# Second attention's stacks loaded as an image from DRAM, and the first expert-choice call's first half routed among the mixture's units

## The reference

```
x = x + 0.5 * mixture(LN(x))          # shared expert + top 2 of 8 experts, silu(g)*u, hidden 256
x = x + linear_attention(LN(x))       # 4 blocks
x = x + 0.5 * mixture(LN(x))          # the same weights again
x = x + 0.5 * expert_choice(LN(x))    # each of 8 experts takes 64 tokens of each sequence
x = x + causal_attention(LN(x))       # 16 heads of 8, rotation by the head's index
x = x + 0.5 * expert_choice(LN(x))
```

## Time and profile before

| | |
|---|---|
| median of 3 runs | 1073.49 us (1071.27 to 1079.22) |
| profiled execution | 1074.08 us |
| its span | 1072.4 us |
| mean granted clock of TensorE | 0.951 |
| busy: PE, DVE, ACT, POOL | 959.2, 706.4, 619.3, 338.7 us |

### The profile page before, as it was taken

One profiled execution on the slowest core, in us unless ns is written; L12 is line 12 of the kernel. 1 busy time (PEld: TensorE's weight loads), 2 busy tenths in 40 slices (PEclk: granted clock), 3 DMA queues, 4 the chain that ended last, 5 costly groups with the idle time before them and its releaser, 6 DMA issues.

```text
span 1072.4 us, 13356 instructions
## 1 busy us (share of the span) xinstructions
PE 959.2 (89%) x4674; PEld 636.4 (59%) x4674; DVE 706.4 (66%) x1413; ACT 619.3 (58%) x1003; POOL 338.7 (32%) x249
## 2 busy tenths in 40 slices
PE   8899999889999999889999998899977878787997
PEld 5678887333333333357888875688544545454886
DVE  3978887577877787546888877634375455438532
ACT  6555555378888888653555553635644545445454
POOL 1697777100000000003777764201201211123200
PEclk9999999999999999888999998899988888889999
DMA  5225120000000000004321211100000000001001
GB/s 173 50 76 162 60 66 23 0 0 1 1 1 1 0 1 1 0 1 135 76 67 59 63 37 60 40 2 1 1 2 2 4 2 2 4 1 40 1 1 40
DMA packets 30745, 33.66 MB, mean 31 GB/s; under 512 B 2063, under 2 KB 19799, under 8 KB 30679
## 3 DMA queue, kind: packets, MB, share of 16 engines
q1 hardware_dynamic: 30678, 32.81, 10.6%
HBM read 31.36 MB, written 1.18 MB: 30 GB/s over the span
## 4 chain that ended last, share of the span: by engine, by line
PE 50%; DVE 20%; ACT 11%; POOL 11%; issue 8%; DMA 0%; SPq 0%; ACTq 0%; POOLq 0%; DVEq 0%
POOL fl L2174 9%; PE ps L128 6%; PE ps L129 6%; PE ps L130 6%; PE ps L760 5%; PE ps L878 4%; PE ps L754 2%; ACT ex L1504 2%; ACT L1393 2%; PE ps L738 2%; DVE smax L2053 2%; PE ps L972 2%; PE ps L907 1%; DVE stk L2045 1%; PE ps L981 1%
## 5 line engine op out<-in xcount | busy, mean ns | idle before, releaser
L2174 POOL TENSOR_TENSOR fl<-fp,fh 128x512 fp32r<-128x512 f32 x144 | 224.1, 1573 | 123.5 <-ACT fh L1299 123.4
L1290 ACT ACTIVATE fs<-ps 128x512 f32<-128x512 f32 x144 | 86.3, 599 | 112.7 <-PE ps L130 112.5
L1762 DVE TENSOR_TENSOR fp<-fp,cwb 128x512 f32<-128x512 f32 x128 | 140.3, 1096 | 14.0 <-DVE fp L1755 0.9
L1755 DVE TENSOR_TENSOR fp<-fs,ps 128x512 f32<-128x512 f32 x144 | 98.1, 682 | 39.4 <-ACT fs L1290 39.0
L128 PE MATMUL ps<-z_hi,w_hi 128*128 128x512 f32 x288 | 116.4, 404 | 3.3 <-DVE fp L1755 3.3
L129 PE MATMUL ps<-z_lo,w_hi 128*128 128x512 f32 x288 | 115.7, 402 | 0.0
L130 PE MATMUL ps<-z_hi,w_lo 128*128 128x512 f32 x288 | 115.2, 400 | 0.0
L1299 ACT CAST fh<-fp 128x512 fp32r<-128x512 f32 x144 | 88.8, 617 | 35.4 <-DVE fp L1762 31.0
L2238 POOL TENSOR_TENSOR ln_sq<-ln_rs 128x512 f32<-128x512 f32 x20 | 21.4, 1069 | 264.8 <-ACT ln_rs L1356 264.8
L2231 POOL TENSOR_SCALAR_AFFINE_SELECT ex<-ex 128x1024 f32<-128x1024 f32 (+1 forms) x24 | 33.4, 1403 | 158.5 <-ACT ex L1504 158.5
L2053 DVE TENSOR_REDUCE smax<-ps 128x8 f32<-128x2048 f32 (+1 forms) x24 | 54.9, 2290 | 42.0 <-PE ps L986 33.9
(11 more groups left out here) (272 smaller groups left out, 2037.1 us busy)
## 6 DMA issues: line engine op xcount, KB each, us to landing
cwb<-cw_spread SPq DMA_DIRECT2D x64, 256.0 KB, 3.1
w_raw<-in_L_ffn_w_dram SPq DMA_DIRECT2D x20, 256.0 KB, 3.1
w_raw<-in_L_ffn_w_dram SPq DMA_DIRECT2D x4, 512.0 KB, 5.7
w<-in_L_ffn_w_dram SPq DMA_DIRECT2D x8, 256.0 KB, 4.8
x_tok<-in_L_attn_x_dram SPq DMA_DIRECT2D x4, 256.0 KB, 3.6
wb<-in_L_attn_W_dram SPq DMA_DIRECT2D x1, 1024.0 KB, 7.0
wb<-in_L_attn_W_dram SPq DMA_DIRECT2D x4, 256.0 KB, 3.9
out_dram<-z SPq DMA_DIRECT2D x4, 256.0 KB, 3.0
```

The costliest lines, as they stand in the source:

```text
L1290: act.activation(fs[:, n % 2, :], ps[:, n % 2, :], ACT.Silu).then_inc(silu_done, 1)
L1755: dve.tensor_tensor(f, fs[:, n % 2, :], ps[:, 2 + n % 2, :], ALU.mult).then_inc(prod_done, 1)
L1762: dve.tensor_tensor(f, f, cwb[:, x % CW_RING, :], ALU.mult).then_inc(weighed, 1)
L2174: pool.tensor_tensor(fl[:, n % RING0, :], fp[:, n % RING0, :], f32(fh[:, n % RING0, :]), ALU.subtract).then_inc(flo_done, 1)
```

## The change

Two parts, and a set-up that the second needs.

1. The routing of the first half of the first expert-choice call moves from the tail into the mixture's units of call 1. With EARLY1 = 47, PE issues the two centrings behind unit 47, the variances behind 50, the scores behind 51, the transposes of the probabilities behind 55, those of the gates and indices behind 67. ACT does one square and copy behind each of 48 and 49, and behind 53 a table load, the exp, and a table load back. DVE does root and weights behind 52, chances behind 54, top_start behind 56, one round behind each of 57 to 64, top_end behind 65, columns behind 68. In the tail the 28 fillers are gone, the two index matmuls stand behind the two turns, and ACT turns the rows of blocks 0 and 1 ahead of the squares of blocks 2 and 3.

2. For blocks 1 to 3 the eight steps are replaced. project_both makes q and k of a block with unscaled weights (wun): two mm3. ACT's both_high writes their high parts (hm), DVE's both_low their low parts (low_qk). SP stores these, as rows, into an image in DRAM (six stores of 256 KB a block: three PARTS for each n), and loads the image into the stack (two loads of 1 MB). The image's constant rows are stored once, from a blank made by POOL in stk[1]. both_high and both_low of blocks 2 and 3 wait until the stores of the block before have landed; plain of a block's first sequence waits for its load. The stores of a block wait for the load of the block before, and a load into a stack waits for the last reads of that stack.

3. In the first expert choice: a re-ordered copy of rope, two matmuls of one column, a copy of the bias and four strided copies 128x128 that make wun from wst.

```diff
+            def store_rows(tb):
+                sp.wait_ge(high_done, 2 * tb)
+                sp.wait_ge(low_done, 2 * tb)
+                if tb == 1:
+                    sp.wait_ge(blank_stored, 16 * 2)
+                else:
+                    sp.wait_ge(stk_loaded, 16 * 2 * (tb - 1))
+                for n in range(2):
+                    for k in range(PARTS):
+                        part = low_qk if k == LOW_PART[n] else hm
+                        sp.dma_start(stk_image[n].rearrange("(g c) h t -> g (c h) t", g=4)[:, HD * HG * k:HD * HG * (k + 1), :],
+                                     f32(part[:, n, :])).then_inc(rows_stored, 16)
+            def load_stack(tb):
+                sp.wait_ge(rows_stored, 16 * 2 * PARTS * tb)
+                if tb >= 2:
+                    sp.wait_ge(t_ready, 3 * SPB * (tb - 1))
+                for n in range(2):
+                    sp.dma_start(f32(stk[tb % 2][:, n]), stk_image[n]).then_inc(stk_loaded, 16)
+            sp.wait_ge(blank_done, 1)
+            for n in range(2):
+                sp.dma_start(stk_image[n], f32(stk[1][:, n])).then_inc(blank_stored, 16)
             for s in range(SEQS):
...
+                if s == 0:
+                    store_rows(1)
+                    load_stack(1)
+                elif s in (1, 3):
+                    store_rows((s + 3) // 2)
+                elif s in (2, 4):
+                    load_stack(s // 2 + 1)
...
+                def project_both(tb):
+                    for n in range(2):
+                        mm3(pe, ps[:, qk_bank(tb, n), :], wun_hi[:, n, :], wun_lo[:, n, :], blk(z_hi, tb), blk(z_lo, tb)).then_inc(both_ready, 1)
...
-                    if first and more:
-                        project_in(tb + 1, range(stack_mid(tb + 1), stack_mid(tb + 1) + 2))
+                    if first and tb + 2 < NTB:
+                        project_both(tb + 2)
...
-                        project_in(1, range(2))
+                        project_both(1)
...
-                    if first and more and tb > 0:
-                        pe.wait_ge(exp_done, 3 * s + 2)
-                        project_in(tb + 1, range(4, 8))
...
+                def both_high(tb):
+                    if tb == 1:
+                        act.wait_ge(stk_done, 2 * HG)
+                    else:
+                        act.wait_ge(rows_stored, 16 * 2 * PARTS * (tb - 1))
+                    for n in range(2):
+                        act.wait_ge(both_ready, 2 * (tb - 1) + n + 1)
+                        act.activation(hm[:, n, :], ps[:, qk_bank(tb, n), :], ACT.Identity, bias=bsu[:, n:n + 1]).then_inc(high_done, 1)
...
-                    if first and more:
-                        stack(tb + 1, range(stack_mid(tb + 1), stack_mid(tb + 1) + 4))
+                    if first and tb + 2 < NTB:
+                        both_high(tb + 2)
...
+                    if call == 1 and n == EARLY1 + 6:
+                        act.preload_act_table_set(LN_EXP)
+                        chances(0, 0)
+                        act.preload_act_table_set("silu_and_others")
...
+                    if call == 1 and n == EARLY1 + 5:
+                        dve.wait_ge(sc_ready, part1(0, 0) + 1)
+                        ln_root(LN_FFN1, 0, SPB - 1)
+                        part_weights(0, LN_FFN1, 0)
+                    if call == 1 and n == EARLY1 + 7:
+                        chances(0, 0)
+                    if call == 1 and n == EARLY1 + 9:
+                        top_start(0, 0)
+                    if call == 1 and n - EARLY1 - 10 in range(CAP // 8):
+                        top_rounds(0, 0, (n - EARLY1 - 10,))
+                    if call == 1 and n == EARLY1 + 18:
+                        top_end(0, 0)
+                    if call == 1 and n == EARLY1 + 21:
+                        columns(0, 0)
...
+                    for half, whole in ((wun_hi, wst_hi), (wun_lo, wst_lo)):
+                        for n in range(2):
+                            own.did(dve.tensor_copy(half[:, n, :].rearrange("p (g r h) -> p g r h", r=HD, h=HG),
+                                                    f32(whole[:, n, :]).rearrange("p (h g c) -> p g c h", h=HG, c=32)[:, :, 0:HD, :]))
...
+                def both_low(tb):
+                    if tb > 1:
+                        dve.wait_ge(rows_stored, 16 * 2 * PARTS * (tb - 1))
+                    for n in range(2):
+                        dve.wait_ge(high_done, 2 * (tb - 1) + n + 1)
+                        dve.scalar_tensor_tensor(out=low_qk[:, n, :], in0=ps[:, qk_bank(tb, n), :], scalar=bsu[:, n:n + 1],
+                                                 in1=f32(hm[:, n, :]), op0=ALU.add, op1=ALU.subtract).then_inc(low_done, 1)
...
+                pool.wait_ge(z_ready, NTB * HALVED.index(LN_ATTN1) + NTB)
+                own.did(pool.memset(f32(stk[1][:, 0]), 0.0))
+                own.wait()
+                own.did(pool.tensor_scalar(stk[1][:, 1], f32(stk[1][:, 0]), rope[:, HG * P + 2:HG * P + 3], None, ALU.add))
+                own.wait()
+                pool.sem_inc(blank_done, 1)
```

More of the change, by code:

```diff
@@ L627, in indices @@
                     pe.wait_ge(ysc_done, n0)
+                elif call == 0 and n == 1:
+                    pe.wait_ge(col_done, part1(call, i) + 1)
                 elif n in (2, 3, 6, 7):
@@ L692, in ffn0 @@
                         down(n - LAG0)
-                    if call == 1 and n == ALL0 - 4:
+                    if call == 1 and n == EARLY1:
                         ln_centre(LN_FFN1, 0)
                         ln_centre(LN_FFN1, 1)
+                    if call == 1 and n == EARLY1 + 3:
+                        pe.wait_ge(lxc_copied, later(LN_FFN1, 1))
+                        ln_variance(LN_FFN1, 0)
+                        ln_variance(LN_FFN1, 1)
+                    if call == 1 and n == EARLY1 + 4:
+                        scores(LN_FFN1, 0)
+                        scores(LN_FFN1, 1)
+                    if call == 1 and n == EARLY1 + 8:
+                        chances(0, 0)
+                    if call == 1 and n == EARLY1 + 20:
+                        tops(0, 0)
                     if n == LAG0 + 1:
@@ L701, in ffn0 @@
                         spare(n % 2, 4)
-                    if call == 1 and n == ALL0 - 4:
-                        pe.wait_ge(lxc_copied, later(LN_FFN1, 1))
-                        ln_variance(LN_FFN1, 0)
-                        ln_variance(LN_FFN1, 1)
-                    if call == 1 and n == ALL0 - 3:
-                        scores(LN_FFN1, 0)
-                        scores(LN_FFN1, 1)
                     if call == 1 and n == ALL0 - 2:
@@ L713, in ffn0 @@
                     rows_turned(0, LN_FFN1, 0)
+                    indices(0, 0)
                     rows_turned(0, LN_FFN1, 1)
+                    indices(0, 1)
                     ln_centre(LN_FFN1, NTB - 1)
@@ L1057, in attn1 @@
                     if 0 <= s < SEQS:
-                        if second and more and tb > 0:
-                            pe.wait_ge(stk_done, (tb + 2) * 2 * HG)
-                        elif s > 0:
+                        if s > 0:
                             pe.wait_ge(exp_done, 3 * s - 1)
@@ L1119, in attn1 @@
                         pe.wait_ge(vaug_done, tb + 2)
-                    if first and more:
-                        pe.wait_ge(stk_done, (tb + 1) * 2 * HG + stack_mid(tb + 1) + 3)
+                    if first and tb + 2 < NTB:
+                        pe.wait_ge(low_done, 2 * (tb + 2))
                     if s + 1 < SEQS:
                         maxima(s + 1)
-                    if s < 0:
-                        for k in range(2, 4):
-                            pe.wait_ge(stk_done, 2 * HG + k - 1)
-                            project_in(1, (k,))
                     if second and tb >= 1:
                         pe.wait_ge(ln_in, u0 + NTB + tb)
-                    if first and more:
-                        pe.wait_ge(stk_done, (tb + 1) * 2 * HG + stack_mid(tb + 1) + 4)
                     if s >= 1:
@@ L1535, in attn1 @@
                     if s < 0:
-                        stack(1, range(2))
-                    if first and more:
-                        stack(tb + 1, range(stack_mid(tb + 1), stack_mid(tb + 1) + 4))
+                        both_high(1)
+                    if first and tb + 2 < NTB:
+                        both_high(tb + 2)
                     if s >= 1:
@@ L1542, in attn1 @@
                         maxima(s + 1)
-                    if s < 0:
-                        stack(1, range(2, 4))
                     if 0 <= s < SEQS:
@@ L1549, in attn1 @@
                         exps(s, 2)
-                    if first and more and tb > 0:
-                        stack(tb + 1, range(4, 8))
                     if s == SEQS - 1:
@@ L2082, in attn1 @@
                         low(tb - 1)
-                    if first and more:
-                        stack(tb + 1, range(stack_mid(tb + 1), stack_mid(tb + 1) + 2))
```

(8 more changed lines are left out.)

89 lines of the change are left out of this document (45 added, 44 removed).

## The result

The changed kernel takes 1084.07 us in the median of 7 runs (1079.93 to 1084.63), before 1074.38 in 7 runs beside it (1071.27 to 1079.22; before's single runs reach from 1065 to 1083 over all the sessions below). The ratio is 1.0072, 95% interval 1.004 to 1.0105: slower, by less than the 1% that was set as the border, though the upper end of the interval lies just beyond it. The profiled execution has a span of 1080.3 us against 1072.4.

What follows compares the result with a forecast made beforehand. TensorE bounds the mixture, a serial VectorE chain the gap, a ring of waits the second attention. Routing +2.0, set-up +1.3 and image -2.6 sum to +0.7: 1074.2 us in terms of the median, range 1058 to 1087.

Steps and rivals of the forecast that it cites:

- part B: Stacks as a DRAM image in the second attention: 9.1 wait, -12.2 gain, 0.5 for later stores and clock; -2.6 us.
- rival of sixteen engines: Second attention's row stores run on sixteen engines, so no wait in s=0; total -9.6, 1063.9 us; chance 0.20.
- slower border: 1084.2 us, about 1% (10.7 us) from no change; a slower result had chance 0.16.
- rivals 3 and 4: 3: mixture units at low clock, 1086 to 1098, chance 0.11; 4: four store engines at 82 GB/s, 1080, chance 0.08.
- sum of +0.7: Whole kernel against the profiled execution: routing +2.0, set-up +1.3, image -2.6 us.
- Stores and s=0, +9.1: Between row maxima of sequences 0 and 1, ACT and DVE wait for six four-engine stores taking 16 us: +9.1 us.
- The ring's gain, -12.2: Second attention's chain of waits between sequences' row maxima: without stack steps, s=2 and s=4 save 4.4 + 1.7 each, -12.2.
- The set-up, +1.3: First expert choice: unscaled-weight copies in DVE's in-order stream delay the next yt that PE awaits; +1.3 us.
- The units, +14.5: Mixture units: added routing exceeds DVE's 0.69 us free per unit; 12.5 plus 2.0 for the last units' fl, 14.5 us.
- The gap, 16.1: Last down of the mixture to first up of the expert choice: 29.3 shrinks to about 16.1, saving 13.2 us.
- part A: Routing moved among the mixture's units: 14.5 added less 13.2 saved in the tail, +1.3, taken as +2.0 us.
- Rival 3: Mixture units with rounds fall to 1.2 GHz after stalls: 1086 for 8 units, 1098 for all 17; chance 0.11.

Runs made afterwards that it cites:

- second kernel of experiment 5: Changed kernel with stores of 32 outer rows; GpSimd's weight halves held until the second half's probabilities are done, four fillers added: 1071.20 us, ratio 0.9967 to before.
- first of experiment 2: Changed kernel with q and k's columns reordered so a store's DRAM side has 32 outer rows instead of four: 1073.57 us, ratio 0.9995 to before.
- the spread half rounds: Changed kernel with stores of 32 outer rows (1073.57), with half a top-8 round per unit and one root step in each of three units: 1073.88 us.
- last kernel of experiment 5: Changed kernel with 32-outer-row stores, weight halves held until the probabilities, four gap fillers, plus three filler runs in the second attention: 1067.28 us, ratio 0.9946 to before.

## Why the prediction was right, and where not

The time lies in the range (1058 to 1087), and the main mechanism of part B, chosen against the rival of sixteen engines, holds: four engines, shown by the end marks, by 102 GB/s, and by the run in which the stores' outermost dimension was changed. But 1074.2 was 10 us too low. The time lies outside the forecast's own 1067 to 1081 and within 0.13 us of the slower border (1084.2). The part of the range that it fell into stood for rivals 3 and 4, and neither of them is what made it up; that it is in the range is in part luck. The sum of +0.7 is +7.9 in the two profiles: +3.3 ahead of the 47th silu, +12.9 in the units behind it, -8.0 in the gap, +1.7 from first up to first row maxima, -3.7 from s=0 to s=6, and +1.8 behind. Term by term:

- **Stores and s=0, +9.1: measured +11.0.** Their first packet came 2.5 us behind the maxima (809.4), as assumed, but they took 17.6 us and not 16. PE, without work meanwhile, came back at a granted clock of 0.50 (824 to 836). PE's timeline of after:

```profile
831.71 0.80 PE L1017 MATMUL ps<-stk 32*128 32x256 f32 x8 [13.13 <-DVE smax L2117]
```

- **The ring's gain, -12.2: measured -14.8 in after's profile, -10.2 in that of the image alone, and -10.2 to -12.5 in those with sixteen engines** (s=2 to s=5, of 86.1 before). The clock moves this term by as much as 4.6 us, and that -12.2 lies in the middle is in part luck. Of the two shares, taken as 6.1 each, s=2 and s=3 gave 3.5 with the image alone and 8.1 in after, s=4 and s=5 6.7 in both. s=5 takes 18.5 us at a granted clock of 0.82 or 16.6 at 1.00; here both with sixteen engines, the second kernel of experiment 5 and the first of experiment 2 (columns as in the earlier trace rows):

```profile
893.75:912.27 18.52, 15.39 (x168) 10.25 (x169) 10.07 (x11) 8.06 (x8) 4.16 (x3) 0.82 0.01 3
895.19:911.75 16.56, 13.02 (x169) 8.58 (x169) 10.02 (x11) 7.96 (x9) 4.16 (x3) 1.00 0.01 3
```

  s=2 and s=3 take 17.5 and 19.1 in after at 0.90 and 0.82, and 20.4 and 20.7 with the image alone at 0.75. The ring as a whole, s=0 to s=6, is -3.7 in after and +1.4 with the image alone, where -2.6 was said.
- **The set-up, +1.3: not to be told from the scatter.** From the weights' low half to the next turned product are 3.3 us instead of 2.4, +0.9, from one row; the four strided copies take 0.25 each, as taken.
- **The units, +14.5: measured +12 to 13** (from the 47th silu to the last down 74.7 to 76.1 us, against 61.9 to 63.5 without early routing; 12.9 between the two main profiles). The stalls came where they were worked out: 2.83 at the root, 0.5 in each unit with a round. One was in no term: PE's own 32 small matmuls for variances and scores (1.95 us at 602.83, 1.85 at 606.83) now stand between full units (in before among the last downs). The size of the free room was argued wrongly all the same: 0.69 us a unit is there only as long as the weighting runs alone, and the spread half rounds showed that it does not.
- **The gap, 16.1: measured 21.3.** This is the step that failed. It took the 8.85 us from root to first up, and the scores at 7.2 us behind the last down, from a tail in which GpSimd's weight halves ran beside the top-8 searches, which they do not slow, and fillers kept PE busy. GpSimd's timeline of before, against the searches of the earlier trace rows:

```profile
659.21 4.94 POOL L2191 TENSOR_TENSOR w_lo<-w_raw,w_hi 128x512 fp32r<-128x512 f32 x4
```

  With the searches gone, the same GpSimd work met the root, and the small matmuls ahead of it ran at 1.2 GHz (granted clock 0.50 over 673 to 677): the root begins 8.7 us behind the last down, and from there to the first up are 12.55. With both taken away, in the last kernel of experiment 5, these are 7.5 and 8.86, as worked out, and the gap is 16.3. So the saving was 8 and not 13, and part A +4 to +5 instead of +2.
- **What no term held:** +1.8 us behind the attention, where the granted clock over the 20 us behind the last row maxima is 0.68 in after and 0.78 in before; the clock there was left out of the sum. Further, the +3.3 ahead of the 47th silu, in stages whose code the change leaves as it is; the first kernel of experiment 2, with the same code there, has +0.5, so this is scatter.

Rival 3 (the units at the low clock) came true for one short stretch only: behind the 2.83 us without work the granted clock is 0.57 over 618 to 622, and it is 0.96 over 600 to 640. The Trainium skill's rule on the number of engines ("DMA: Bandwidth & Descriptors", section "Why a DMA increments its semaphore by 16 and not by 1") agrees with both row stores: 128 against 4 gives four end marks, 128 against 32 sixteen.

The parts do not add up: alone +7.0 and +8.1 in the medians, together +9.7. The early routing leaves the image kernel only 3.6 to 3.8 us slower (1084.07 for 1080.52, 1073.57 for 1069.73), while on before it costs 8.1, with an interval of its own of 0.2 to 1.1%. Its gap and units are alike in all of them. The profiles show where the clock adds or takes: s=2 and s=3 are 4.6 us shorter in after than with the image alone, by the same code, and the routing alone loses 2.9 us behind the attention. One profile of each kernel does not say how often that happens, so for the medians it is an inference and not shown.

## What to carry to other kernels

Look at the outermost dimension of both sides of a DMA before counting on its rate: four blocks of 32 rows and 32 rows of four blocks were the same bytes, at 102 and some 380 GB/s. Work moved into an engine's idle time has room only for what that idle time is when its neighbours run too; and the work that is left behind meets what the moved work had kept away. Where work is taken from TensorE in a ring of short waits, look at its granted clock next: part of what the ring gained was lost there, and a few fillers in the waits brought some of it back (1069.73 to 1065.42 us).

## What the runs showed of the hardware that was not expected

DVE's top-8 searches keep their 0.41 us beside GpSimd's tensor operations (also in the units), while arithmetic on 128x8 elements beside the same operations took 1.19 us instead of 0.17 in three operations of the second half's root (the two ahead of them, 0.17 and 0.26, escaped). The weighting from SBUF took 1.0 to 1.6 us beside fl and 0.69 when the units had become long enough for the two to miss each other. Two executions of one program, before, differ by 2.1 us at the last down and by 1.2 in s=0, the latter at a granted clock of 0.89 and 0.69.
